# A butterfly FFN behind a gated scan on one core: the down side's high product as whole 128x512 products, its result regrouped by 32 on-chip copies, and one token load issued later

## The chip, the cores and the metric

One Trainium2 chip, one of its cores. The metric is the device time of one execution of the program in microseconds (us), lower is better. The profiled execution gives a time of its own, and a span from its first to its last instruction; all positions in time below count from the start of that span.

## The reference, cut to what matters

```python
# x, ctx: (32, 512, 512) f32; hidden width 2048, 11 butterfly stages
x = x + layernorm(x) * scan(ctx * ctx)            # r = 0.9 * r + kv, along the sequence
h = layernorm(x) @ W_exp + b_exp                  # 512 -> 2048
h = butterfly(h, up_weights)                      # 11 stages of 2x2 blocks, strides 1 .. 1024
h = gelu(h + up_bias)
h = butterfly(h, down_weights)                    # 11 stages
x = x + (h @ W_con + b_con) + down_bias           # 2048 -> 512
```

A butterfly over 2048 features is a low part (7 stages with strides under 128: 16 blocks of 128x128, one a block of features) times a high part (4 stages with strides 128 to 1024, which mix the 16 blocks). Neither depends on the tokens, so the program multiplies both into the weights once, at its start, and then runs all tokens through two dense products.

## The kernel before

**The fold.** The first 140 us make the two dense weight matrices. For the down side the source is `W_con`, loaded into the tile `wcon` as 16 slices `r` of 128 rows (row `(k, e)` of slice r is the feature of block k with rank r and place e within it). Three kinds of fold step work on it, each on TensorE (PE) into one of four PSUM banks in turn, and each followed by an eviction on ScalarE (ACT), line 995:

- `high_dn` r = 0..15 (line 1818): four products with 128x128 output each, of slice r of `wcon` with the high matrix `HX[:, 1, r]`. The result comes out transposed, and the eviction scatters it into the tile `Z`.
- `back` k = 0..15 (line 1824): four 128x128 transposes each that turn block k of `Z` back, evicted into `wcon[:, k]` (two of them on VectorE, DVE, line 1345).
- `low_dn` i = 0..15 (line 1803): one 128x512 product of block `W2_ORDER[i]` of `wcon` with the low matrix `LX[:, 1]`. ACT (line 992) and DVE (line 1341) split the result in two parts, which SyncE (SP) stores to DRAM (line 634) as the tensor `w2_split`.

Between them stand small steps: `tokens` 0..7 (line 1822, transposes of the normalised first tokens, evicted into `raw`), `bias_low` (line 1792), `turn_low` (line 1820, evicted into `LX`). A fold step may begin when the step four before it has been evicted, since it takes its bank.

**The splits of the up side.** `weights_hi(0)` and `weights_hi(1)` on ACT (line 1022) and `weights_lo` on DVE (line 1350) split the first two pairs of up-side weights; SP stores them in three groups each (`store_w1`, line 623). ACT waits for the stores of groups 0 and 1 of the first before it evicts `tokens` 0 (their staging tile lies over `raw`).

**The tokens.** `tokens_hi(0, m)` on ACT (line 1040) and `tokens_lo(0, m)` on DVE (line 1445) split the tokens of product m of 7 into the tile `xop`; `token_sum` (DVE, line 1462) makes the sums for four of them. The tile `xop` lies over the region of `Z`: slot 4 and up of it are used early.

**The steady state.** 32 units of 1024 tokens, each of 8 pairs p; a pair is 7 products m of 6 matmuls (line 1916, a Strassen-like scheme) with down products between (lines 1937, 1950), in an order written out by hand. In unit 0 the products of pair 0 are woven with the last `low_dn` steps, and pairs 2 to 7 take their up weights from "late" loads (lines 655, 656), which are split on ACT and GpSimd (POOL) and stored for the later units. SP issues nearly all transfers, in program order: a wait in it holds all that stands behind. In pair 1 of unit 0 it loads the token rows of unit 1 into `x` (`load_x`, two halves of 1 MB, four transfers each).

Of the kernel before, what the change touches and what calls it, by code (L numbers as in the profile page):

```python
# [24 lines left out]
def xattn_ffn_program(nc, x_in, ctx_in, w_exp, b_exp, up_w, up_bias, down_w, w_con, b_con, down_bias, out):  # L25
# [6 lines left out]
    P = 128  # L32
# [4 lines left out]
    LOW = 7  # L37
# [19 lines left out]
    XORDER = (0, 1, 3, 2, 5, 4, 6)  # L57

# [6 lines left out]
    W2_ORDER = (2, 3, 4, 5, 6, 7, 12, 13, 8, 1, 9, 0, 14, 10, 11, 15)  # L65
    W2_USE = [(i, 0) for i in range(14)] + [(3, 1), (14, 0)]
# [16 lines left out]
    with es:  # L83
# [122 lines left out]

        low_loaded = [sem("low_up_loaded"), sem("low_dn_loaded")]
# [118 lines left out]
        FOLD += [("high_dn", r, "act") for r in range(4)]  # L326
        FOLD += [("bias_low", 0, "act")]
        FOLD += [("high_dn", r, "act") for r in range(4, 8)]
        FOLD += [("bias_turn", 0, "act")]
        FOLD += [("high_dn", r, "act") for r in range(8, R - 3)]  # L330
        FOLD += [("tokens", i, "act") for i in range(2)]
        FOLD += [("high_dn", r, "act") for r in range(R - 3, R)]
        FOLD += [("tokens", i, "act") for i in range(2, J)]
        FOLD += [("turn_low", q, "act") for q in range(KH // 4)]
        FOLD += [("back", k, "act") for k in range(10)]
        FOLD += [("tokens", i, "act") for i in range(J, J + 2)]
        FOLD += [("back", k, "dve" if k in (11, 13) else "act") for k in range(10, KH)]
        FOLD += [("tokens", i, "dve") for i in range(J + 2, 2 * J)]


        FOLD += [("low_dn", k, "dve") for k in range(KH)]
# [78 lines left out]
        Zd = Z[:, :, :].rearrange("p a b -> p (a b)").rearrange("p (c h) -> p c h", c=KD)  # L420

        def kept(kind, i, bank):
# [13 lines left out]
            if kind == "turn_high":  # L436
                return HX[:, 1, 4 * i:4 * i + 4, :].rearrange("p a b -> p (a b)"), whole
# [6 lines left out]
            if kind == "tokens":  # L444
                return raw[:, i // J, :, :].rearrange("p c (g j i) -> p c g j i", g=G, j=J)[:, :, :, i % J, :],\
                    whole.rearrange("p (c g i) -> p c g i", c=KD, g=G)
            assert kind == "back"
            return wcon[:, i, :], whole
# [121 lines left out]
        def _(sp):  # L570
# [48 lines left out]
            def store_w1(n):  # L619
                p = W1_ORDER[n]  # L620
                for g, (m0, m1) in enumerate(GROUPS):
# [19 lines left out]
            store_w1(0)  # L641
# [44 lines left out]
            def load_x(u, par):  # L686
                wait(sp, out_stored, (u - 1) * (2 * G * NX))
                for h in range(2):
                    load_tokens(xs[par], h, x_rows, u * 2 + h, x_loaded[h])

            def body(u, par, first, last):
# [4 lines left out]
                for p in range(NP):  # L696
# [3 lines left out]
                    for m in range(NM):  # L700
# [29 lines left out]
                        if go and p == 1 and m == 5:  # L730
# [3 lines left out]
                            load_x(u + 1, 1 - par)  # L734
# [245 lines left out]
        def _(act):  # L980
# [43 lines left out]
            def tokens_hi(u, m, first):  # L1024
                if not first:
                    act.wait_ge(m_done, u * PER + (m + 1 - NM))
                if m in (0, 1):
                    if first:
                        act.wait_ge(fold_made, fold_at("back", KH - 1) + 1)
# [10 lines left out]
                act.activation(xop[:, XPOS[m], 0, :, :], x_source(m), ACT.Copy).then_inc(xhi_ready, 1)  # L1040
# [48 lines left out]
            fold_step("high_dn", 3)  # L1089
            fold_step("bias_low", 0)  # L1090
            for r in range(4, 8):
                fold_step("high_dn", r)
            fold_step("bias_turn", 0)
            for r in range(8, 12):
                fold_step("high_dn", r)
            fold_step("high_dn", 12)
            for group in range(2):
                act.wait_ge(w1_stored[0][group], NX)
            for i in range(2):
                fold_step("tokens", i)  # L1100
            for r in range(13, R):
                fold_step("high_dn", r)
            for i in range(2, J):
                fold_step("tokens", i)
            for q in range(KH // 4):
                fold_step("turn_low", q)
            for k in range(4):
                fold_step("back", k)
            for k in range(4, 10):
                fold_step("back", k)  # L1110
            for i in range(J, J + 2):
                fold_step("tokens", i)
            for k in (10, 12, 14, 15):
                fold_step("back", k)
            tokens_hi(0, 0, True)
            tokens_hi(0, 1, True)
            for k in range(4):
# [123 lines left out]
        def _(dve):  # L1241
# [73 lines left out]
            def top_products(dn):  # L1315
                dve.wait_ge(path_product, spreads(dn, LOWS - 1))
                for c, bank in enumerate(TOP_PLACE[dn]):
# [3 lines left out]
                    if dn:  # L1321
                        last = nc.vector.tensor_tensor(
                            out=whole.rearrange("p o (r a e) -> p o a e r", r=R, a=2),
                            in0=paths.rearrange("p (o e r) -> p o e r", o=KH // 4, r=R).unsqueeze(2)
                            .to_broadcast([P, KH // 4, 2, E // 2, R]),
                            in1=coef.rearrange("p o a (e r) -> p o a e r", r=R), op=ALU.mult)
                    else:
                        last = path_stage(nc.vector, flat(whole), paths, coef, LOW - 1)
# [114 lines left out]
            def tokens_lo(u, m):  # L1443
                dve.wait_ge(xhi_ready, u * NM + (XPOS[m] + 1))
                nc.vector.tensor_tensor(out=xop[:, XPOS[m], 1, :, :], in0=x_source(m),  # L1445
# [601 lines left out]
```

## Time and profile before

| | |
|---|---|
| time before, median of 3 runs | 2752.51 us (2751.94 to 2758.26) |
| the profiled execution: its time / its span | 2752.11 us / 2750.4 us |
| PE busy (matmul) | 2728.7 us, 99% of the span |
| DVE, ACT, POOL busy | 2119.6, 1132.2, 427.1 us |
| granted TensorE clock, mean | 0.996 of full |
| DMA | 535.76 MB, 195 GB/s over the span |

A share of busy time is an average over stages. The fold (up to 142 us) has other limits than the rest, and it is the part that the change touches, so it is read by itself: by stretches, and by the order of the instructions on each engine.

### The profile page before, as it was taken

The numbers are of one execution on the slowest core, as the hardware profiler recorded it, in microseconds if no ns is written. First come the engines' busy times: TensorE is split into PE (matmuls) and PEld (weight loads), VectorE is DVE, ScalarE is ACT, GpSimd is POOL, SyncE is SP. The second block draws the span as 40 slices with busy tenths as digits, with TensorE's granted clock in tenths as the row PEclk, the third lists the DMA queues.
The fourth block names the chain that finished last, engine by engine and source line by source line (L and its number), as shares of the span: only waits on it lengthen the run. The fifth ranks groups of instructions, "written<-read, shape, count | busy, mean of one in ns | idle before, by whom it ended". The sixth has DMA issues, their size and how long they took to land.

```text
span 2750.4 us, 35138 instructions
## 1 busy us (share of the span) xinstructions
PE 2728.7 (99%) x12168; PEld 2251.9 (82%) x12168; DVE 2119.6 (77%) x3544; ACT 1132.2 (41%) x1731; POOL 427.1 (16%) x608
## 2 busy tenths in 40 slices
PE   8999999999999999999999999999999999999998
PEld 6788888888888888888888888888888888888887
DVE  8888887877878777787877788787787877778533
ACT  5754434344343433434343343434334343343432
POOL 5356010110101011020111101011010101102000
PEclk8999999999999999999999999999999999999999
DMA  9675956657585675857657585675758567585543
GB/s 274 244 235 171 281 165 198 200 170 224 155 231 177 181 220 161 241 153 216 194 168 222 152 249 165 194 202 171 223 156 235 172 189 213 161 242 153 187 146 100
DMA packets 288373, 535.76 MB, mean 195 GB/s; under 512 B 36854, under 2 KB 98454, under 8 KB 271046
## 3 DMA queue, kind: packets, MB, share of 16 engines
q1 hardware_dynamic: 281808, 531.05, 64.1%
q10 hardware_dynamic: 5414, 1.25, 0.3%
q8 instruction: 99, 1.62, 0.2%
q0 software_dynamic: 976, 1.22, 0.2%
q14 instruction: 76, 0.62, 0.1%
HBM read 437.96 MB, written 63.96 MB: 182 GB/s over the span
## 4 chain that ended last, share of the span: by engine, by line
PE 98%; DVE 1%; ACT 0%; issue 0%; DMA 0%; POOL 0%; DVEq 0%
PE ps L1916 44%; PE ps L1937 25%; PE ps L1950 25%; PE ps L1814 1%; PE ps L1710 1%; PE ps L1782 0%; PE ps L1818 0%; PE ps L1812 0%; PE ps L1824 0%; DMA wexp<-in_L_ffn_W_exp_dram 0%; PE ps L2022 0%; PE ps L1803 0%; DVE raw L1462 0%; DVE xop L1445 0%; PE ps L1729 0%
## 5 line engine op out<-in xcount | busy, mean ns | idle before, releaser
L1916 PE MATMUL ps<-xop,w1r 128*128 128x512 f32 x5376 | 1366.1, 389 | 2.4 <-DVE xop L1445 2.4
L1916 PEld LDWEIGHTS ps<-xop,w1r 128*128 128x128 f32 x5376 | 1009.0, 188 | 215.2 <-DVE xop L1445 3.4
L1937 PE MATMUL ps<-w2r,ghi 128*128 128x512 f32 x2048 | 630.5, 389 | 0.0
L1950 PE MATMUL ps<-w2r,ghi 128*128 128x512 f32 x2032 | 625.7, 389 | 1.1 <-DVE x L1544 1.1
L1127 ACT ACTIVATE st<-ps 128x512 f32<-128x512 f32 x384 | 229.6, 598 | 820.0 <-PE ps L1916 819.9
L1544 DVE TENSOR_TENSOR x<-ps,x 128x512 f32<-128x512 f32 x508 | 348.4, 686 | 275.1 <-PE ps L1950 272.7
L1937 PEld LDWEIGHTS ps<-w2r,ghi 128*128 128x128 f32 x2048 | 384.4, 188 | 79.9 <-DVE w2x L1341 0.2
L1950 PEld LDWEIGHTS ps<-w2r,ghi 128*128 128x128 f32 x2032 | 381.3, 188 | 81.0 <-DVE x L1544 2.0
L1562 DVE TENSOR_TENSOR g<-ps,st 128x512 f32<-128x512 f32 x384 | 262.5, 684 | 211.7 <-PE ps L1916 211.7
L1131 ACT ACTIVATE g<-g,gelu_bias 128x512 f32<-128x512 f32 x384 | 275.5, 717 | 353.0 <-DVE g L1562 352.9
L1567 DVE TENSOR_TENSOR glo<-g,ghi 128x512 fp32r<-128x512 f32 x510 | 350.9, 708 | 72.8 <-ACT ghi L1145 72.8
L1937 PE MATMUL ps<-w2r,glo 128*128 128x512 f32 x1024 | 398.3, 389 | 0.0
L1950 PE MATMUL ps<-w2r,glo 128*128 128x512 f32 x1016 | 395.2, 389 | 0.0
L1145 ACT ACTIVATE ghi<-g 128x512 fp32r<-128x512 f32 x512 | 309.8, 629 | 12.2
L1138 ACT ACTIVATE g<-ps,gelu_bias 128x512 f32<-128x512 f32 x128 | 88.2, 689 | 349.0 <-PE ps L1916 349.0
L1937 PEld LDWEIGHTS ps<-w2r,glo 128*128 128x128 f32 x1024 | 192.3, 188 | 39.8
L1950 PEld LDWEIGHTS ps<-w2r,glo 128*128 128x128 f32 x1016 | 190.8, 188 | 39.5
L836 POOL TENSOR_TENSOR x<-x,bias_row 128x512 f32<-128x512 f32 x128 | 170.0, 1332 | 244.2 <-DVE kvT L1434 218.8
L819 POOL TENSOR_TENSOR ve<-mv,eps 128x4 f32<-128x4 f32 x32 | 12.2, 382 | 1197.2 <-DVE mv L1385 1197.2
L1371 DVE TENSOR_TENSOR_SCAN kvT<-decay,kvT 128x512 f32<-128x512 f32 x128 | 159.1, 1243 | 4.4
L1445 DVE TENSOR_TENSOR xop<-raw,xop 128x1024 fp32r<-128x1024 f32 x112 | 136.6, 1232 | 0.7 <-ACT xop L1040 0.7
L827 POOL TENSOR_TENSOR ve<-mv,eps 128x1 f32<-128x1 f32 x128 | 28.2, 220 | 597.8 <-DVE mv L1413 597.8
(182 smaller groups left out, 1700.0 us busy)
## 6 DMA issues: line engine op xcount, KB each, us to landing
w1r<-w_products SPq DMA_DIRECT2D x847, 256.0 KB, 3.3
w2r<-w_split SPq DMA_DIRECT2D x126, 1024.0 KB, 5.0
x<-in_x_dram SPq DMA_DIRECT2D x128, 256.0 KB, 7.0
raw<-kv SPq DMA_DIRECT2D x480, 64.0 KB, 2.1
out_dram<-x SPq DMA_DIRECT2D x120, 256.0 KB, 4.1
kv<-in_ctx_dram SPq DMA_DIRECT2D x64, 256.0 KB, 7.4
raw<-in_ctx_dram SPq DMA_DIRECT2D x64, 256.0 KB, 5.0
w_products<-w1r SPq DMA_DIRECT2D x43, 256.0 KB, 6.9
```

Of the source, the lines that this page charges most:

```text
L836: nc.gpsimd.tensor_tensor(out=x[:, J * h + j, :], in0=x[:, J * h + j, :], in1=bias_row[:, :], op=ALU.add).then_inc(bias_added, 1)
L1127: act.activation(st[:, i, :], bank[:, :], ACT.Copy).then_inc(copied, 1)
L1131: act.activation(g32[:, q, :], g32[:, q, :], ACT.Gelu, bias=gelu_bias[:, k:k + 1])\
L1145: act.activation(ghi[:, p % 2, q, :], g32[:, q, :], ACT.Copy).then_inc(ghi_ready, 1)
L1371: nc.vector.tensor_tensor_scan(out=flat, data0=decay[:, :], data1=flat, initial=0.0, op0=ALU.mult, op1=ALU.add).then_inc(scanned, 1)
L1445: nc.vector.tensor_tensor(out=xop[:, XPOS[m], 1, :, :], in0=x_source(m), in1=xop[:, XPOS[m], 0, :, :].bitcast(f32), op=ALU.subtract).then_ ...
L1544: nc.vector.tensor_tensor(out=x[:, J + j, :], in0=ps_yb[:, :], in1=x[:, J + j, :], op=ALU.add)\
L1562: nc.vector.tensor_tensor(out=by_chunk(g32[:, q, :]), in0=by_token(bank[:, :]), in1=by_token(st[:, i, :]), op=ALU.add).then_inc(h_ready, 1)
L1567: nc.vector.tensor_tensor(out=glo[:, p % 2, q, :], in0=g32[:, q, :], in1=ghi[:, p % 2, q, :].bitcast(f32), op=ALU.subtract).then_inc(glo_r ...
L1916: last = nc.tensor.matmul(bank[:, :], w1r[:, slot, w, c * P:(c + 1) * P], xop[:, XPOS[m], v, c, :], start=(opens and i == 0), stop=(i == l ...
L1937: last = nc.tensor.matmul(ps_ya[j][:, :], g[:, p % 2, q, j * P:(j + 1) * P], w2r[:, p % 2, kk, w, :], start=(p == 0 and kk == 0 and i == 0 ...
L1950: last = nc.tensor.matmul(ps_yb[:, :], g[:, p % 2, q, j * P:(j + 1) * P], w2r[:, p % 2, kk, w, :], start=(kk == 0 and i == 0), stop=(kk == ...
```

## The change

The four 128x128 products of a `high_dn` step become one 128x512 product with the operands the other way round, so its result is not transposed any more, and is evicted as it is into `Z[:, r]`. The 16 `back` steps with their evictions are gone. What `back` did to the places of the rows is done by DMA: for each r one copy takes 64 partitions of `Z[:, r]` (half the blocks; 2 KB of each partition, 128 KB in all) to 8 partitions r, r+16, ... of `wcon`, 8 blocks of 2 KB each. There are 32 such copies on SP's queue: 16 for blocks 0 to 7 (after `high_dn` 7 has read its slice and step r has been evicted), and 16 for blocks 8 to 15 (after `high_dn` 15). `low_dn` 0 waits for the first 16, `low_dn` 6 for the other 16. The stores of the first pair's up weights are taken apart: group 1 after nine copies, group 2 after all 32.

`tokens` 0..7 are all evicted by ACT now; `bias_low` and `bias_turn` come after all `high_dn`; the first three `tokens_hi` come earlier on ACT. The slots of `xop` are dealt out anew (`XSLOT`), and the slots over `Z` wait for its copies.

Apart from that, the second half of `load_x` in unit 0 is issued at m = 3 of pair 2 instead of at m = 5 of pair 1, so behind the stores and loads of late weights that stand between.

```diff
     XORDER = (0, 1, 3, 2, 5, 4, 6)
+    XSLOT = (5, 6, 1, 0, 3, 2, 4)
...
+    LOW_BLOCKS_FIRST = 6
...
             if kind == "high_dn":
-                return Zd[:, :, :].rearrange("p c (k r e) -> p c k r e", k=KH, r=R)[:, :, :, i, :],\
-                    whole.rearrange("p (c k e) -> p c k e", c=KD, e=E)
+                return Z[:, i, :], whole
...
+            def move_dn(blocks, r, moved):
+                wait_kept(sp, "high_dn", r)
+                sp.dma_start(wcon[r:P:R, blocks, :], Z[blocks.start * E:blocks.stop * E, r, :]).then_inc(moved, NX)
...
-            store_w1(0)
+            store_w1(0, range(1))
+            sp.wait_ge(fold_made, fold_at("high_dn", R // 2 - 1) + 1)
+            for r in range(R):
+                move_dn(slice(0, KH // 2), r, dn_low_moved)
+                if r == R // 2:
+                    store_w1(0, range(1, 2))
+            sp.wait_ge(fold_made, fold_at("high_dn", R - 1) + 1)
+            for r in range(R):
+                move_dn(slice(KH // 2, KH), r, dn_top_moved[r // 4])
+            store_w1(0, range(2, NG))
...
-                            load_x(u + 1, 1 - par)
+                            load_x(u + 1, 1 - par, range(1) if first else range(2))
+                        if first and p == 2 and m == 3:
+                            load_x(u + 1, 1 - par, range(1, 2))
...
+                if first and XSLOT[m] < R // 4:
+                    act.wait_ge(dn_low_moved, R * NX)
+                    act.wait_ge(dn_top_moved[XSLOT[m]], 4 * NX)
+                if first and m == 6:
+                    act.wait_ge(w1_stored[0][2], NX)
...
                 if kind == "low_dn":
                     k = W2_ORDER[i]
-                    wait_kept(pe, "back", k)
+                    if i == 0:
+                        pe.wait_ge(dn_low_moved, R * NX)
+                    if i == LOW_BLOCKS_FIRST:
+                        for moved in dn_top_moved:
+                            pe.wait_ge(moved, 4 * NX)
...
+                if kind == "high_dn":
+                    nc.tensor.matmul(bank[:, :], HX[:, 1, i, :], wcon[:, i, :], start=True, stop=True).then_inc(fold_made, 1)
+                    return
...
                 if first:
-                    for k in range(4):
+                    for k in range(2, 4):
                         fold_step("low_dn", k)
                     product(u, 0, 0, first)
-                    for k in range(4, 6):
-                        fold_step("low_dn", k)
                     product(u, 0, 1, first)
-                    for k in range(6, 8):
+                    for k in range(4, 8):
                         fold_step("low_dn", k)
                     product(u, 0, 2, first)
```

On PE, from the `high_dn` steps to the first `low_dn`, the order before (`HX,wcon` are `high_dn`, `ident,Z` are `back`, `wcon,LX` are `low_dn`, `ident,kv` are `tokens`, `ident,LX` are `turn_low`, `LX,scr` is `bias_low`):

```order
L1818 MATMUL ps<-HX,wcon 128x128 x16
L1792 MATMUL ps<-LX,scr 16x128 x16
L1818 MATMUL ps<-HX,wcon 128x128 x16
L1798 MATMUL ps<-ident,scr 128x16
L1818 MATMUL ps<-HX,wcon 128x128 x20
L1822 MATMUL ps<-ident,kv 128x128 x8
L1818 MATMUL ps<-HX,wcon 128x128 x12
L1822 MATMUL ps<-ident,kv 128x128 x8
L1820 MATMUL ps<-ident,LX 128x128 x16
L1824 MATMUL ps<-ident,Z 128x128 x40
L1822 MATMUL ps<-ident,kv 128x128 x8
L1824 MATMUL ps<-ident,Z 128x128 x24
```

The same place of the changed program (`wcon,HX` are `high_dn`):

```order
L1800 MATMUL ps<-wcon,HX 128x512 x16
L1816 MATMUL ps<-ident,kv 128x128 x16
L1781 MATMUL ps<-LX,scr 16x128 x16
L1814 MATMUL ps<-ident,LX 128x128 x16
L1787 MATMUL ps<-ident,scr 128x16
L1796 MATMUL ps<-wcon,LX 128x512 x2
L1816 MATMUL ps<-ident,kv 128x128 x16
L1796 MATMUL ps<-wcon,LX 128x512 x2
L1899 MATMUL ps<-xop,w1r 128x512 x12
L1796 MATMUL ps<-wcon,LX 128x512 x4
L1899 MATMUL ps<-xop,w1r 128x512 x6
```

The 64 transposes of `back` are gone, all `high_dn` stand in one run, and the last four `tokens` have moved behind the first two `low_dn`. After the third product the order is as before.

On SP, from the store of the folded up weights to the first store of `w_split`, before:

```order
L639 DMA w_folded<-W1f 128x3072 x2
L623 DMA w_products<-w_first 128x2x512
L623 DMA w_products<-w_first 128x512
L623 DMA w_products<-xop 128x4x512
L609 DMA w1r<-w_products 128x512
L623 DMA w_products<-w1r 128x2x512
L623 DMA w_products<-w1r 128x512
L623 DMA w_products<-w1r 128x4x512
L634 DMA w_split<-w2s 128x2x512
```

and in the changed program:

```order
L636 DMA w_folded<-W1f 128x3072 x2
L620 DMA w_products<-w_first 128x2x512
L613 DMA wcon<-Z 8x8x512 x9
L620 DMA w_products<-w_first 128x512
L613 DMA wcon<-Z 8x8x512 x23
L620 DMA w_products<-xop 128x4x512
L601 DMA w1r<-w_products 128x512
L620 DMA w_products<-w1r 128x2x512
L620 DMA w_products<-w1r 128x512
L620 DMA w_products<-w1r 128x4x512
L631 DMA w_split<-w2s 128x2x512
```

The 32 copies stand between the stores, and every later transfer of the fold is queued behind them.

## Rows read from the trace of the kernel before

**Rows 1.** The page: span, busy time of each engine.

```profile
span 2750.4 us, 35138 instructions
PE 2728.7 (99%) x12168; PEld 2251.9 (82%) x12168; DVE 2119.6 (77%) x3544; ACT 1132.2 (41%) x1731; POOL 427.1 (16%) x608
```

**Rows 2.** Stretches of the start: busy time by engine, granted clock, DMA share, GB/s.

```profile
core 0: us, PE busy (x) PEld busy (x) DVE busy (x) ACT busy (x) POOL busy (x), PEclk, DMA share, GB/s
79.00:101.00 22.00, 21.37 (x187) 20.41 (x187) 21.25 (x36) 17.06 (x34) 11.14 (x13) 1.00 0.82 314
101.00:112.00 11.00, 11.00 (x92) 9.71 (x91) 5.55 (x12) 10.74 (x22) 6.45 (x28) 1.00 0.01 1
112.00:142.00 30.00, 26.73 (x85) 15.12 (x84) 27.18 (x34) 21.41 (x36) 6.34 (x4) 1.00 0.79 266
```

**Rows 3.** PE from 79 to 142 by line: count | busy us, mean ns | idle.

```profile
L1803 PE MATMUL ps<-wcon,LX 128*128 128x512 f32 x32 | 15.3, 602 | 0.8 <-DVE w2s L1341 0.6
L1818 PE MATMUL ps<-HX,wcon 128*128 128x128 f32 x128 | 15.2, 277 | 0.2 <-ACT HX L995 0.2
...
L1824 PE MATMUL ps<-ident,Z 128*128 128x128 f32 x64 | 7.8, 281 | 0.0
L1822 PE MATMUL ps<-ident,kv 128*128 128x128 f32 x32 | 4.3, 276 | 0.0
L1792 PE MATMUL ps<-LX,scr 128*16 128x128 f32 x32 | 3.7, 273 | 0.4 <-ACT Z L995 0.4
```

**Rows 4.** PE in order of time: start, us, line, count [idle before it].

```profile
79.30 3.81 PE L1818 MATMUL ps<-HX,wcon 128*128 128x128 f32 x32 [0.22 <-ACT HX L995]
...
96.48 2.84 PE L1818 MATMUL ps<-HX,wcon 128*128 128x128 f32 x24
...
111.12 3.60 PE L1803 MATMUL ps<-wcon,LX 128*128 128x512 f32 x8
...
119.70 1.12 PE L1803 MATMUL ps<-wcon,LX 128*128 128x512 f32 x2
...
127.46 3.59 PE L1803 MATMUL ps<-wcon,LX 128*128 128x512 f32 x8
130.89 0.29 PE L1983 MATMUL ps<-scr 128*128 128x16 f32 x2
...
139.64 1.61 PE L1916 MATMUL ps<-xop,w1r 128*128 128x512 f32 x6
...
211.16 0.73 PE L1950 MATMUL ps<-w2r,ghi 128*128 128x512 f32 x2 [0.46 <-DVE x L1544]
```

**Rows 5.** ACT in order of time, two evictions of high_dn steps.

```profile
82.88 1.55 ACT L995 ACTIVATE Z<-ps 128x512 f32<-128x512 f32 x3
...
87.03 0.58 ACT L995 ACTIVATE Z<-ps 128x512 f32<-128x512 f32 x1
```

**Rows 6.** DVE in order of time: first token_sum; statistics of the second half.

```profile
114.36 1.22 DVE L1462 TENSOR_TENSOR raw<-raw 128x1024 f32<-128x1024 f32 x1
...
215.72 2.46 DVE L1392 BATCH_NORM_STATS2 st<-x 128x6 f32<-128x512 f32 x4
```

**Rows 7.** DMA rates of three stretches, columns as in rows 2.

```profile
82.00:84.00 2.00, 1.59 (x15) 1.35 (x15) 1.93 (x3) 2.00 (x4) 1.92 (x2) 1.00 1.05 442
...
157.00:166.00 9.00, 9.00 (x41) 7.44 (x41) 8.79 (x15) 5.78 (x9) 2.58 (x3) 1.00 1.07 246
...
262.00:272.00 10.00, 10.00 (x45) 8.29 (x45) 5.96 (x7) 5.40 (x11) 8.68 (x7) 1.00 0.43 110
```

**Rows 8.** SP's queue: start, us spent issuing, transfer, count.

```profile
261.86 10.69 SPq L566 DMA_DIRECT2D raw<-kv  x16
```

**Rows 9.** DMA issues: KB each, median us from issue to landing.

```profile
raw<-kv SPq DMA_DIRECT2D x480, 64.0 KB, 2.1
```

**Rows 10.** Two stretches early in the start-up, columns as in rows 2.

```profile
12.00:14.00 2.00, 0.29 (x3) 0.05 (x1) 2.00 (x3) 2.00 (x5) 2.00 (x2) 1.00 1.11 289
...
17.00:24.00 7.00, 7.00 (x24) 5.38 (x23) 6.38 (x11) 4.43 (x6) 7.00 (x17) 0.53 1.10 223
```

More of the change, by code:

```diff
@@ L205, in xattn_ffn_program @@
         ps_f = ps[5:8]
+        dn_low_moved = sem("dn_low_moved")
+        dn_top_moved = [sem(f"dn_top_moved{q}") for q in range(R // 4)]
         low_loaded = [sem("low_up_loaded"), sem("low_dn_loaded")]
@@ L325, in xattn_ffn_program @@
         FOLD += [("turn_high", q, "act") for q in range(R // 4)]
-        FOLD += [("high_dn", r, "act") for r in range(4)]
+        FOLD += [("high_dn", r, "act") for r in range(R)]
+        FOLD += [("tokens", i, "act") for i in range(J)]
         FOLD += [("bias_low", 0, "act")]
-        FOLD += [("high_dn", r, "act") for r in range(4, 8)]
+        FOLD += [("turn_low", q, "act") for q in range(KH // 4)]
         FOLD += [("bias_turn", 0, "act")]
[L330 to L341, printed above, removed]
+        FOLD += [("low_dn", k, "dve") for k in range(2)]
+        FOLD += [("tokens", i, "act") for i in range(J, 2 * J)]
+        FOLD += [("low_dn", k, "dve") for k in range(2, KH)]
         kept_count, kept_so_far = [], {"act": 0, "dve": 0}
@@ L418, in w1_columns @@
             return w[:, :, :, r * E:(r + 1) * E].rearrange("p k c e -> p c k e")
-        Zd = Z[:, :, :].rearrange("p a b -> p (a b)").rearrange("p (c h) -> p c h", c=KD)
         def kept(kind, i, bank):
@@ L443, in kept @@
                     whole.rearrange("p (a e r) -> p a r e", a=4, e=E)
[L444 to L448, printed above, removed]
+            assert kind == "tokens"
+            return raw[:, i // J, :, :].rearrange("p c (g j i) -> p c g j i", g=G, j=J)[:, :, :, i % J, :],\
+                whole.rearrange("p (c g i) -> p c g i", c=KD, g=G)
         def w2_slot(i):
@@ L1320, in top_products @@
                     coef = spread_view(ps[bank][:, :], 0, LOW - 1, KH // 4)
[L1321 to L1328, printed above, removed]
+                    last = path_stage(nc.vector, flat(whole), paths, coef, LOW - 1)
                 last.then_inc(low_matrix_ready, 1)
@@ L1507, in _ @@
                 normalise(0, 1, xs[0], j)
-            for k in (11, 13):
-                fold_step("back", k)
-            for i in range(J + 2, 2 * J):
-                fold_step("tokens", i)
             tokens_lo(0, 0)
             tokens_lo(0, 1)
-            token_sum(0, 0, first=True)
             for k in range(2):
                 fold_step("low_dn", k)
+            token_sum(0, 0, first=True)
             token_sum(0, 1)
@@ L1877, in _ @@
                 fold_step("turn_low", q)
-            wait_kept(pe, "high_dn", R - 2)
-            wait_kept(pe, "high_dn", R - 1)
-            for k in range(KH):
-                if k == 10:
-                    for i in range(J, J + 2):
-                        fold_step("tokens", i)
-                fold_step("back", k)
-            for i in range(J + 2, 2 * J):
+            fold_step("bias_turn", 0)
+            wait_kept(pe, "turn_low", KH // 4 - 1)
+            for k in range(2):
+                fold_step("low_dn", k)
+            for i in range(J, 2 * J):
                 fold_step("tokens", i)
-            wait_kept(pe, "turn_low", KH // 4 - 1)
             def product(u, p, m, first):
```

67 lines of the change are left out of this document (23 added, 44 removed).

## The prediction

> **What bounds the kernel now.** I read the page first, then the stretches of the start, then each engine there in order of time. PE is busy for 99% of the span [rows 1], so the steady state gives and takes nothing: whatever this change does happens in the start-up, where the fold runs. By stretches [rows 2], PE works 21.4 of 22 us from 79 to 101 and all of 101 to 112, so PE itself is the limit there; from 112 to 142 it works 26.7 of 30, with DVE at 27.2 of 30, so there DVE sets the pace. The DMA engines are idle from 101 to 112 (share 0.01) and loaded on both sides of it (0.82 and 0.79). The marks on PE to hold a new schedule against are [rows 4]: first `high_dn` at 79.30, last one done at 96.48 + 2.84 = 99.3, `low_dn` 0 at 111.12, `low_dn` 6 at 119.70, first product of pair 1 at 139.64. The change of the last mark is the change of the kernel's time, unless something behind it stalls.
>
> **What PE loses and gains.** By the groups of lines [rows 3], the 64 transposes of `back` cost 7.8 us and go. The 64 small `high_dn` products cost 15.2 us. Sixteen 128x512 products replace them; four `low_dn` products of that shape take 130.89 - 127.46 = 3.43 us [rows 4], 0.857 us each, so 13.7 us. The ceiling of the gain is 7.8 + 1.5 = 9.3 us.
>
> The steps are now packed tighter than their evictions come. Step 4 needs the bank of step 0, whose eviction begins at 82.88 behind `weights_hi(0)` and ends near 83.4 [rows 5], while PE would be ready at 79.30 + 3.43 = 82.7: a wait of 0.7 us. Step 7 needs the eviction of step 3, which stands behind `weights_hi(1)` and ends at 87.03 + 0.58 = 87.6 [rows 5]; PE is ready at 83.4 + 2.6 = 86.0: 1.6 us. Then nine steps at 0.857: the last `high_dn` ends at 95.3, 4.0 us earlier than before. With durations from [rows 3], four `tokens` (half of 4.3 us for eight, less where they are pipelined, 1.8) end at 97.1, `bias_low` (3.7) at 100.8, `turn_low` (some 1.9) at 102.7; its last eviction on ACT stands behind a `tokens_hi` and ends near 104.3. So without any wait for copies `low_dn` 0 starts at 104.3, 6.8 us early. Then come two `low_dn` (1.7) and the last four `tokens` (1.8) with their evictions; the first `token_sum` on DVE can start near 108.8, where it starts at 114.36 now [rows 6]. From there DVE has the same list as before, and it is the limit, so 5.5 us is what arrives at pair 1.
>
> **The copies.** There are 32, of 128 KB each, on SP's queue, 4.2 MB in all. The first can be issued once step 7 is made, at 87.6 + 0.9 = 88.5. A copy of this kernel from SBUF to SBUF (`raw<-kv`, 64 KB, 32 partitions to 32) lands 2.1 us after its issue [rows 9]; its transfer is 0.27 us of that (below), so 1.8 us is fixed. On SP one such issue costs 10.69 / 16 = 0.67 us [rows 8]; 32 take 21 us, to about 110.
>
> How long the transfer of one copy takes is shown by no row, and the whole case hangs on it. The nearest rows [rows 7]: transfers over 128 partitions move 442 GB/s at a DMA share of 1.05; loads of token rows into 32 partitions at a time, among others, move 246 GB/s at a share of 1.07; the `raw<-kv` copies move 110 GB/s at a share of 0.43, so 10 x 0.43 / 16 = 0.27 us of all engines for 64 KB. At 442 GB/s a copy takes 0.30 us, the lower bound. Like `raw<-kv` it takes 0.54 us. The rows also say that at a full share the rate halves nearly (442 to 246) when a transfer writes 32 partitions in place of 128. A copy here writes 8. If the rate halves once more (123 to 110 GB/s) a copy takes 1.06 to 1.2 us; if it falls in proportion to the partitions (62 GB/s) 2.1 us, the upper bound. The form of the access (8 target partitions, in steps of 16) is further from `raw<-kv` than that is from a full tile, so I take a further halving, at its slow end, 1.2 us.
>
> The Trainium skill, page "SBUF — State Buffer", section "Door 1: The DMA port swizzle", says that SBUF is reached through 16 ports, chosen by bits 2 to 4 and 6 of the partition number, each about 27 GB/s. By it the targets r, r+16, ... of one copy reach four ports, some 109 GB/s, 1.2 us a copy; the row of `raw<-kv` would have 0.54 us and the kernel 5.5 us faster, the page has it slower. The loads into 32 partitions in the trace agree with it (8 ports), and no row here shows four. The page "DMA: Bandwidth & Descriptors", section "Why a DMA increments its semaphore by 16 and not by 1", adds that a transfer is split over as many engines as divide its outermost sizes, here 8; that alone would make 0.6 us.
>
> **Who waits for them.** At 1.2 us a copy, with the 256 KB store of group 1 between them (0.65 us at 400 GB/s):
> - Group 1 lands at 88.5 + 1.8 + 9 x 1.2 + 0.65 = 101.8. ACT waits for it ahead of the eviction of `tokens` 0, and PE's `bias_low` for that bank: `bias_low` from 102.3 to 106.0, `turn_low` evicted at 109.5.
> - The low 16 land at 88.5 + 1.8 + 19.2 + 0.65 = 110.2: `low_dn` 0 starts there, 0.9 us earlier than before.
> - The top 16 land at 110.2 + 19.2 = 129.4. `low_dn` 6 waits for all of them; PE reaches it at about 120 and stands for 9 us, and behind it stand products 2 to 6 and all other `low_dn`, while DVE runs out of work.
> - From `low_dn` 6 to pair 1 the order is unchanged and takes 139.64 - 119.70 = 19.9 us now, 0.6 of it a wait that falls away [rows 4]: 19.3. Pair 1 starts at 129.4 + 19.3 = 148.7, 9.1 us later than now.
>
> Each 0.1 us on a copy moves this by 3.2 us. The two chains (copies; PE and DVE) meet at 0.9 us a copy for no change, and below 0.72 the 5.5 us are kept whole.
>
> Two smaller terms. The group 2 store, the stores of the second pair's weights and 16 stores of `w_split` (8.4 MB) start after the copies, at 129 and not at 116, with pair 1 only 9 us later; the loads of late weights behind them lose some 4 us of their lead. And PE stands still for 9 us: in the start-up PE was busy for 0.3 us of 12 to 14, and over 17 to 24 the granted clock was 0.53 [rows 10], so mostly the lower of its two levels (1.2 of 2.4 GHz); the same over a few us of this dense stretch costs 1 to 3 us. I add 2 us for both (0 to 5).
>
> **The second edit.** Four 256 KB transfers move from behind the first half in pair 1 to behind the late loads of pair 2. With pair 1 at 148.7 and a pair of 20 us (three and a half of them from 139.64 to 211.16 [rows 4]) they are issued near 177. DVE reads this half at 215.72 [rows 6], 39 us after that, so it costs nothing; if that cover were gone it would cost the 4.3 us that 1 MB takes at 246 GB/s [rows 7]. It frees the queue for the split weights and late weights of pairs 2 and 3, which is worth something only if PE waits for them; the one PE wait in that part is 0.46 us, for DVE [rows 4]. I take 0.
>
> **Sum**, against the profiled execution (2752.11 us, span 2750.4 [rows 1], 1.7 us outside it): 2752.1 + 9.1 + 2 = 2763.2. The median of the runs is 2752.51, so I say 2763. About 0.3% (8.3 us, so 2760.8 and 2744.3) is what a measurement here tells from no change.
>
> **Rivals.**
> - *The copies are quick enough* (up to 0.72 us, like `raw<-kv`, or only half the engines' rate). For it: that row is the one on-chip copy in the trace; against it: eight target partitions. Then `low_dn` 0 is at 104.3, `low_dn` 6 near 114.5 with the top copies landed at 88.5 + 1.8 + 32 x 0.67 + 0.65 = 112.4, and the time 2752.1 - 5.5 = 2746.6. Decides below 0.9 us a copy. Chance 0.34.
> - *In between* (0.8 to 1.0 us): 2749 to 2756. Chance 0.12.
> - *The backlog decides*: as forecast, but the queue behind the copies starves pairs 1 and 2 (split and late weights land late), or a copy takes 1.4 us and more. For it: the DMA engines have a share of 1.07 from 157 to 166 already [rows 7]. Then 8 us and more on top: 2771 and up. Chance 0.10.
> - *The forecast*: copies of 1.06 to 1.28 us, small terms 0 to 5: 2757 to 2769. Chance 0.44.
>
> **The numbers.** The forecast's own range lies above 2760.8 for about six sevenths: slower 0.38 + 0.10 = 0.48. Faster by over 8.3 us needs nearly the whole ceiling of 9.3 us and no new wait: 0.04. The rest, 0.48, is within. To hold eight in ten the range goes from the quick case (2745) to the foot of the backlog case (2771).
>
> **What would show it.** The 16 `high_dn` products end near 95.3 in any case, with two waits of 0.7 and 1.6 us for ACT among them. SP issues the copies from 88.5 at 0.6 to 0.7 us. In the stretch 92 to 108 the DMA rate is 100 to 125 GB/s if I am right, over 180 if the quick case holds. `low_dn` 0 starts near 110 (or 104), and PE's longest wait of the start is at `low_dn` 6, some 9 us (or none). Pair 1 starts at 148.7 to 151 (or near 134). I am wrong if copies overlap where I have them share a limit, or if the stores between them were the real wait.

## The result, and the profile of the changed kernel

The changed kernel takes 2763.69 us (median of 5 runs, 2762.59 to 2765.66); the kernel before, on the same chip, 2751.94 us (5 runs, 2751.2 to 2758.26). The ratio is 1.0039, with a 95% interval of 1.0025 to 1.0054: 11.8 us slower, where 2763 was forecast. The profiled execution has a span of 2762.0 us.

TensorE in order of time, the changed kernel (start, us, line, count, idle before it in brackets; line 1800 is `high_dn`, 1816 `tokens`, 1781 `bias_low`, 1796 `low_dn`, 1899 the products of the tokens; each `low_dn` step leaves two records, so x4 is two steps):

```profile
78.16 3.67 PE L1800 MATMUL ps<-wcon,HX 128*128 128x512 f32 x8 [0.22 <-ACT HX L1003]
82.71 2.81 PE L1800 MATMUL ps<-wcon,HX 128*128 128x512 f32 x6 [0.87 <-ACT Z L1003]
87.06 7.96 PE L1800 MATMUL ps<-wcon,HX 128*128 128x512 f32 x18 [1.54 <-ACT Z L1003]
94.86 1.91 PE L1816 MATMUL ps<-ident,kv 128*128 128x128 f32 x16
102.95 5.82 PE L1781 MATMUL ps<-LX,scr 128*16 128x128 f32 x32 [6.18 <-ACT raw L1003]
...
111.99 1.98 PE L1796 MATMUL ps<-wcon,LX 128*128 128x512 f32 x4 [1.16 <-ACT scr L1003]
...
128.94 3.75 PE L1796 MATMUL ps<-wcon,LX 128*128 128x512 f32 x4 [6.70 <-DMA wcon<-Z]
133.87 2.93 PE L1899 MATMUL ps<-xop,w1r 128*128 128x512 f32 x6 [1.18 <-DVE xop L1438]
...
137.52 2.24 PE L1899 MATMUL ps<-xop,w1r 128*128 128x512 f32 x6
...
144.59 1.66 PE L1899 MATMUL ps<-xop,w1r 128*128 128x512 f32 x6 [1.27 <-DVE xop L1438]
...
151.79 1.63 PE L1899 MATMUL ps<-xop,w1r 128*128 128x512 f32 x6
```

The last row is the first product of pair 1. It stood at 139.64 [rows 4]; it is 12.15 us later, and the whole kernel 11.8 us: in this kernel all of the loss arises in the start, none of it behind. The row of 128.94 is `low_dn` 6, which stands 6.70 us for the copies. And the engine is slow behind it: two `low_dn` steps (four records) take 3.75 us there, and 1.98 at 111.99.

The rows alone could mislead on the other large wait, 6.18 us ahead of `bias_low`. The row of ACT that it waits for, and SP's queue over the same time:

```profile
102.30 2.06 ACT L1003 ACTIVATE raw<-ps 128x512 f32<-128x512 f32 x4 [6.64 <-DMA w_products<-w_first]
```

```profile
88.19 5.89 SPq L613 DMA_DIRECT2D wcon<-Z  x9
94.12 0.56 SPq L620 DMA_DIRECT2D w_products<-w_first  x1
94.74 18.23 SPq L613 DMA_DIRECT2D wcon<-Z  x23
113.02 0.83 SPq L620 DMA_DIRECT2D w_products<-xop  x1
```

The store of group 1 is issued at 94.12, but ACT, which waits for it, starts only at 102.30: nine copies are ahead of it. Experiment 9 shows that this wait costs nothing.

By stretches (columns as in [rows 2]), the changed kernel:

```profile
79.00:101.00 22.00, 15.36 (x47) 7.15 (x45) 21.01 (x37) 13.22 (x24) 11.59 (x14) 0.99 0.63 206
...
96.00:100.00 4.00, 0.77 (x8) 0.53 (x5) 3.82 (x8) 0.00 (x0) 3.08 (x4) 1.00 0.53 105
104.00:108.00 4.00, 4.00 (x23) 2.93 (x22) 1.22 (x1) 1.42 (x2) 0.00 (x0) 0.58 0.53 116
108.00:112.00 4.00, 2.84 (x26) 2.32 (x23) 1.23 (x1) 3.19 (x7) 0.00 (x0) 1.00 0.53 121
124.00:128.00 4.00, 0.00 (x0) 0.00 (x0) 0.00 (x0) 0.00 (x0) 0.00 (x0) 0.56 0.87 265
128.00:132.00 4.00, 3.06 (x4) 1.17 (x4) 0.00 (x0) 0.98 (x2) 0.00 (x0) 0.50 0.97 375
132.00:136.00 4.00, 2.82 (x6) 1.75 (x6) 3.41 (x4) 1.54 (x3) 0.00 (x0) 0.50 1.05 371
136.00:142.00 6.00, 6.00 (x16) 3.35 (x16) 3.45 (x6) 3.38 (x5) 0.00 (x0) 0.82 0.98 365
142.00:160.00 18.00, 16.71 (x65) 11.58 (x64) 14.20 (x20) 13.46 (x22) 6.35 (x4) 1.00 1.02 320
```

The copies move 105 to 121 GB/s at a DMA share of 0.53. 131,072 bytes at these rates are 1.25 to 1.08 us a copy; by the landing, (128.94 - 88.19 - 1.8 - 0.65) / 32 = 1.20 us. The share says that the 16 engines as a whole are half free in the stretches from 96 to 112, in which the copies run nearly alone. It doesn't say so any more while TensorE waits at `low_dn` 6 (0.87 from 124 to 128, at 265 GB/s): by then the stores and loads behind the copies are moving as well. After TensorE's wait the granted clock is 0.50, the lower level (1.2 GHz), until about 138.

### The profile page after: what moved, and what is told of

Same layout as the page of the kernel before. It is cut to its first block, busy times and chain, and to the rows that moved or that the text cites. A ratio compares the mean times of both kernels' runs of the same rounds, so it can differ in the third digit from the quotient of the medians.

```text
span 2762.0 us, 34825 instructions
## 1 busy us (share of the span) xinstructions
PE 2726.1 (99%) x12008; PEld 2238.6 (81%) x12008; DVE 2115.7 (77%) x3540; ACT 1126.5 (41%) x1719; POOL 431.7 (16%) x608
## 3 DMA queue, kind: packets, MB, share of 16 engines
q10 hardware_dynamic: 5414, 1.25, 0.3%
## 4 chain that ended last, share of the span: by engine, by line
PE 97%; DMA 1%; ACT 0%; DVE 0%; POOL 0%; issue 0%; SPq 0%; ACTq 0%; DVEq 0%
PE ps L1899 44%; PE ps L1920 25%; PE ps L1933 25%; DMA wcon<-Z 1%; PE ps L1699 1%; PE ps L1810 1%; PE ps L1771 0%; DMA w_products<-w_first 0%; PE ps L1808 0%; PE ps L1796 0%; PE ps L1800 0%; PE ps L1781 0%; PE ps L2003 0%; DMA wexp<-in_L_ffn_W_exp_dram 0%; PE ps L1718 0%
## 5 line engine op out<-in xcount | busy, mean ns | idle before, releaser
L827 POOL TENSOR_TENSOR ve<-mv,eps 128x4 f32<-128x4 f32 x32 | 11.8, 369 | 1198.0 <-DVE mv L1378 1198.0
```

## The experiments

The theory: a copy takes 1.2 us because its 8 target partitions, in steps of 16, are written at some 110 GB/s; the landing of the last 16 holds `low_dn` 6, and from there to pair 1 the order takes its 19.9 us and some for the clock. Its rivals: the wait for the store of group 1 is the loss; the copies share a limit that has nothing to do with the targets (8 engines, SP's issues); the queue behind them is what costs. Ratios are to the kernel before on the same chip.

**1 and 2: each edit alone.** The second edit alone is the kernel before with

```diff
-                            load_x(u + 1, 1 - par)
+                            load_x(u + 1, 1 - par, range(1) if first else range(2))
+                        if first and p == 2 and m == 3:
+                            load_x(u + 1, 1 - par, range(1, 2))
```

> The kernel before with the second edit alone: the second half of unit 1's token rows is issued at m = 3 of pair 2 behind the late weights. My account: no effect, within 1 us of the kernel before (2752), pair 1 starts at 139 to 140 as before, and no new wait of PE. Rival (the second edit carries part of the 12 us, because the load then collides with the loads of late weights): 2754 to 2764 and new PE waits between 142 and 230.

2751.86 us, ratio 0.9995 (0.9986 to 1.0004): nothing. The copies alone are the changed kernel with these lines turned back.

> The changed kernel without the second edit: only the fold is changed. My account: all of the loss is in the fold, so the time is that of the changed kernel, 2762 to 2765, with PE's wait of 6 to 7 us for the top copies. Rival (the second edit is needed to keep the token rows from the late weights once the queue is 13 us behind): over 2766, with PE waits in pairs 1 to 3. Other rival (the second edit costs): below 2760.

2769.8 us (2765.53 to 2771.07), ratio 1.0059 (1.0046 to 1.0073). Pair 1 starts where it does with both edits (151.22), so the other 5.7 us (17.4 against 11.8 over before) are lost behind it. The profile of the copies alone is of an execution of 2765.53 us, the quickest of the five, and shows only a part of that: TensorE is busy for 18.35 of 20 us from 180 to 200, in pair 2 (all 20 in the changed kernel), and ahead of that stands ACT's wait for the late weights that are queued behind the two megabytes of token rows:

```profile
188.87 0.73 ACT L1154 ACTIVATE w1r<-late_top 128x256 fp32r<-128x256 f32 x2 [6.69 <-DMA late_low<-w_folded]
```

So the second edit is worth nothing by itself and 5.7 us in this kernel.

**3: half the bytes.** Each copy moves the first 1 KB of each row and not the 2 KB, so half of the down side's weights is not regrouped (its product is not the reference's); the count of copies stays.

```diff
-                sp.dma_start(wcon[r:P:R, blocks, :], Z[blocks.start * E:blocks.stop * E, r, :]).then_inc(moved, NX)
+                sp.dma_start(wcon[r:P:R, blocks, 0:D // 2], Z[blocks.start * E:blocks.stop * E, r, 0:D // 2]).then_inc(moved, NX)
```

> The changed kernel with the 32 copies moving only the first 1 KB of each 2 KB row (half of what low_dn then reads is left as loaded from W_con). Same count of copies, same issue time on SP, same waits. If the transfer time of the copies is what holds PE (1.16 us a copy), it falls to about 0.6 us, no wait for the top copies is left, and the time is 2745 to 2750. If SP's issuing (0.6 us each) or a fixed cost of each copy is what counts, the copies end no more than a few us earlier and the time stays at 2758 or above.

2749.98 us, ratio 0.9988 (0.9979 to 0.9997). No wait for copies is left, and pair 1 starts at 136.42, 3.2 us earlier than before. The bytes are the cost, not the number of issues. And the best that the idea has to give, with half of its transfers for nothing, is 2.4 us.

**4 and 5: other target partitions.** In steps of 4, with the columns of the low matrix in the matching order, so that the result is the same product:

```diff
-                sp.dma_start(wcon[r:P:R, blocks, :], Z[blocks.start * E:blocks.stop * E, r, :]).then_inc(moved, NX)
+                at = Q * (r % 4) + r // 4
+                sp.dma_start(wcon[at:at + Q - 3:4, blocks, :], Z[blocks.start * E:blocks.stop * E, r, :]).then_inc(moved, NX)
```

> The changed kernel with each copy's eight target partitions in steps of 4 and not of 16 (rows of each block stored in another order, and the low matrix written in the same order by the DVE operation that makes it): same bytes, same count of copies, of rows and of target partitions. If the targets share ports by pairs (four ports for steps of 16, eight for steps of 4), a copy takes about 0.6 us, DMA rate 200 to 220 GB/s in the stretch of the copies, low_dn 0 starts near 104, no long wait for the top copies, and the time is 2745 to 2749, faster than both kernels. If the limit is the number of target partitions or the source side (64 partitions), nothing changes: 105 to 120 GB/s and 2762 to 2765.

2753.31 us, ratio 1.0002 (0.9993 to 1.0011). The stretches of this kernel:

```profile
104.00:108.00 4.00, 3.17 (x26) 2.52 (x24) 1.75 (x2) 2.85 (x6) 0.00 (x0) 0.96 0.51 180
108.00:112.00 4.00, 3.58 (x19) 2.33 (x20) 1.38 (x2) 2.59 (x7) 3.13 (x18) 1.00 0.51 182
...
142.00:160.00 18.00, 16.15 (x71) 12.76 (x70) 11.99 (x19) 9.16 (x15) 6.77 (x8) 1.00 1.04 322
```

180 GB/s in place of 116 to 121, at the same share: as much of the DMA engines is held, for a shorter time (0.73 us a copy). The wait at `low_dn` 6 is gone and pair 1 starts at 138.25. TensorE then loses 1.85 us in 142 to 160 that the kernel before doesn't lose.

Side by side, with the regrouped product in the wrong order:

```diff
-                sp.dma_start(wcon[r:P:R, blocks, :], Z[blocks.start * E:blocks.stop * E, r, :]).then_inc(moved, NX)
+                sp.dma_start(wcon[E * r:E * (r + 1), blocks, :], Z[blocks.start * E:blocks.stop * E, r, :]).then_inc(moved, NX)
```

> The changed kernel with each copy written to 8 partitions side by side (8r to 8r+7) in place of 8 in steps of 16; the same bytes, source, count of copies, and queue. The regrouped product is then in the wrong order, so the output is not the reference's; the work on every engine is the same. Theory 1, the place of the targets sets the rate of a copy: side by side they reach fewer ports than in steps of 16 (by the Trainium skill, page "SBUF - State Buffer", section "Door 1: The DMA port swizzle", two, 54 GB/s), so a rate of 50 to 60 GB/s in the stretch 96 to 112 at the same share of 0.53, some 2.3 us a copy, the top copies landed near 88.5 + 1.8 + 32 x 2.3 + 0.65 = 165 and pair 1 at 165 + 20 to 23 = 185 to 188, the kernel some 35 us slower than the changed one (2795 to 2802). Theory 2, the number of target partitions (8) sets it, or that 8 of the 16 engines do the work: 105 to 121 GB/s as in the changed kernel, and 2763 to 2765.

2776.93 us in its one run. The stretches of this kernel:

```profile
104.00:108.00 4.00, 0.00 (x0) 0.00 (x0) 0.07 (x1) 0.00 (x0) 0.00 (x0) 0.50 0.54 68
...
112.00:116.00 4.00, 4.00 (x20) 2.87 (x19) 1.23 (x1) 1.65 (x3) 0.00 (x0) 0.50 0.54 93
```

`low_dn` 6 starts at 142.87, (142.87 - 89.13 - 1.8 - 0.65) / 32 = 1.60 us a copy; 62 to 68 GB/s in the stretches from 92 to 108 that hold no store, 93 to 94 from 112 to 124. The place of the targets does set the rate, in the direction expected, but 2.3 us was too much, and why the rate rises from 68 to 93 on the way was not found. One reading is that neighbouring copies overlap where their targets differ enough. That became the tenth experiment.

**6: TensorE kept busy.** Eight products more, thrown away, ahead of the wait at `low_dn` 6:

```diff
+                        for _ in range(8):
+                            nc.tensor.matmul(ps_yb[:, :], LX[:, 1, k, :], wcon[:, W2_ORDER[0], :], start=True, stop=True)
```

> The changed kernel with 8 products of 128x512 (results thrown away) on TensorE between low_dn 5 and the wait of low_dn 6. Theory 1, of the 22.9 us from low_dn 6 to pair 1 (19.3 at the pace of before) some 3 us are the granted clock of 0.50 after the wait: busy for 6.9 of the 6.7 us of the wait, the engine keeps a clock near 1, low_dn 6 starts no later (129 to 130), pair 1 at 148.5 to 149.5 in place of 151.8, and the kernel 2760 to 2762. Theory 2, the 3 us come from something else (ACT or DVE behind late stores): the clock after low_dn 6 is higher, but pair 1 stays at 151 to 152 and the time at 2763 to 2764. If the products run at the lower clock themselves they take up to 14 us and low_dn 6 starts up to 7 us later: then the time is over 2765 and the run tells nothing on the clock.

2763.94 us, ratio 1.0043 (1.0029 to 1.0056): no difference from the changed kernel that can be told. In its profile the clock is 1.00 when `low_dn` 6 starts, at 131.29 (the whole start stands later, first `high_dn` at 79.94), and pair 1 follows 21.55 us later, not 22.85. So 1.3 of the 3 us over 19.9 go with the clock of the first steps. The clock falls again, to 0.50 from 136 to 138, after TensorE has waited 2.03 us for DVE:

```profile
131.29 1.96 PE L1798 MATMUL ps<-wcon,LX 128*128 128x512 f32 x4 [0.45 <-DMA wcon<-Z]
135.28 2.53 PE L1901 MATMUL ps<-xop,w1r 128*128 128x512 f32 x6 [2.03 <-DVE xop L1438]
...
138.53 2.29 PE L1901 MATMUL ps<-xop,w1r 128*128 128x512 f32 x6
```

The same two products in the kernel before:

```profile
123.72 1.67 PE L1916 MATMUL ps<-xop,w1r 128*128 128x512 f32 x6 [1.16 <-DVE xop L1445]
...
125.68 1.94 PE L1916 MATMUL ps<-xop,w1r 128*128 128x512 f32 x6
```

From the start of the one to the start of the other it is 1.96 us before, 3.25 us here and 3.65 in the changed kernel, with no wait between in any of them. So most of the rest is the lower clock too.

**7 and 8: what remains with quick copies.** With steps of 4, the store of group 1 ahead of all copies:

```diff
-            store_w1(0, range(1))
+            store_w1(0, range(2))
...
-                if r == R // 2:
-                    store_w1(0, range(1, 2))
```

> The kernel with target partitions in steps of 4 (2753.3), and the store of group 1 issued ahead of the copies, no longer between them. Theory 1, that store's place costs ACT its 2.7 us wait ahead of bias_low: the wait is gone, low_dn 0 starts at 105 to 106 in place of 108.3, and if nothing else holds, pair 1 at 135.5 in place of 138.25 and the kernel 2750 to 2751. Theory 2, the DMA queue behind the copies is the limit by then (a share of 1.04 from 116 to 160): low_dn 0 is early all the same, but the 2.7 us are given back at ACT's wait for the context rows and DVE's behind it (142 to 165), and the kernel stays at 2752.5 to 2754.

2753.24 us, ratio 1.0004 (0.9995 to 1.0013). And on top of it, the loads of unit 1's context rows ahead of the first five stores of `w_split`; its old place in pair 0 is empty:

```diff
             store_w1(1)
+            sp.wait_ge(fold_made, fold_at("tokens", 2 * J - 1) + 1)
+            load_tokens(kv, 0, ctx_rows, 2, ctx_loaded[0])
             for i in range(5):
                 store_w2(i)
```

> As the kernel with steps of 4 and the store first, and the four loads of unit 1's context rows issued ahead of the first five stores of w_split, not behind ten of them. Theory 1, what is left of the loss is that ACT waits 3.7 us for these rows at 144.8: the wait falls below 1 us, PE's waits at 153 and 160 (1.8 us) shrink, and the kernel is 1 to 3 us faster than the one with the store first (2748 to 2751). Theory 2, the queue as a whole is late, so that whichever transfer stands last is waited for: then the first five w_split stores land 4 us later, DVE and ACT wait for their buffers from 120 to 140, and the time is the same or up to 3 us worse.

2752.85 us, ratio 1.0003 (0.9994 to 1.0012). ACT in the kernel with the store first, and then in the one with the context rows earlier too:

```profile
145.28 1.92 ACT L1006 ACTIVATE kv<-kv 128x2048 f32<-128x2048 f32 x1 [4.51 <-DMA kv<-in_ctx_dram]
...
151.45 0.72 ACT L1130 ACTIVATE g<-g,gelu_bias 128x512 f32<-128x512 f32 x1 [3.77 <-DMA w_split<-w2s]
```

```profile
135.10 0.18 ACT L1190 ACTIVATE gelu_bias<-ps 128x16 f32<-128x16 f32 x1 [3.49 <-DMA w_split<-w2s]
```

The wait of 4.51 us for the context rows is gone in the second, and the wait for `w_split` stands at 135 and not at 151; TensorE, which started pair 1 at 137.87 in the first, starts it at 141.93 here. The time is the same. That is how a full queue looks (DMA share 0.97 to 1.05 from 116 to 160 in both): putting one transfer ahead makes another the late one.

**9: the store of group 1 first, slow copies.** The two edits of the diff of the seventh, in the changed kernel:

> The changed kernel with the store of group 1 issued ahead of the copies, targets in steps of 16 as in the change. Theory 1, only the landing of the top copies decides: the wait ahead of bias_low (6.2 us) is gone, low_dn 0 waits for the low copies instead, until about 109, the wait at low_dn 6 stays near 6.7 us or grows, and the top copies land at the same place (128 to 129, 0.65 us earlier at most): the time stays at 2762.5 to 2764. Theory 2, the 6.2 us wait of ACT and TensorE ahead of bias_low is part of the loss: pair 1 starts up to 6 us earlier (146 to 148) and the time is 2757 to 2759.

2764.22 us, ratio 1.0043 (1.0029 to 1.0056), as the changed kernel. TensorE:

```profile
97.53 3.67 PE L1779 MATMUL ps<-LX,scr 128*16 128x128 f32 x32
...
110.86 3.75 PE L1794 MATMUL ps<-wcon,LX 128*128 128x512 f32 x4 [7.61 <-DMA wcon<-Z]
...
129.17 3.75 PE L1794 MATMUL ps<-wcon,LX 128*128 128x512 f32 x4 [5.97 <-DMA wcon<-Z]
```

The 6.18 us ahead of `bias_low` are gone, and 7.61 us at `low_dn` 0 have taken their place; `low_dn` 6 starts at 129.17 as at 128.94. Of two waits in a row, the one that ends last counts. Pair 1 is at 150.05 in this profile, 20.88 us behind `low_dn` 6 and not 22.85: the granted clock was back at 1.00 by 134 to 136 here, where it was 0.50 until 138 in the changed kernel.

**10: the same copies in another order.** The changed kernel with

```diff
-            for r in range(R):
+            turns = [8 * a + b + c for a in range(2) for b in range(4) for c in (0, 4)]
+            for n, r in enumerate(turns):
                 move_dn(slice(0, KH // 2), r, dn_low_moved)
-                if r == R // 2:
+                if n == R // 2:
...
-            for r in range(R):
+            for r in turns:
                 move_dn(slice(KH // 2, KH), r, dn_top_moved[r // 4])
```

> The changed kernel with the copies issued in the order r = 0, 4, 1, 5, 2, 6, 3, 7, 8, 12, 9, 13, 10, 14, 11, 15 in both halves and nothing else: each copy has the same bytes, shape and targets as before. By the port rule of the Trainium skill (page "SBUF - State Buffer", section "Door 1: The DMA port swizzle") copies r and r + 4 write to different ports, copies r and r + 1 (r in the same four) to the same ones. Theory 1, what sets the rate is which ports are written at one time, and neighbouring copies overlap: 150 to 180 GB/s in the stretch 96 to 112, some 0.75 us a copy, no wait at low_dn 6, pair 1 near 138 to 140 and the kernel at 2752 to 2755. Theory 2, each copy by itself is held to the rate of its own four ports, or to something in its shape that the order doesn't change: 105 to 121 GB/s, a wait of 6 to 7 us at low_dn 6, 2763 to 2764.

2754.42 us, ratio 1.0007 (0.9998 to 1.0016): some 10 us of the 11.8 are back, and nothing but the order of 32 issues has changed. Stretches and the place of `low_dn` 6 and pair 1 in this kernel:

```profile
92.00:96.00 4.00, 4.00 (x11) 1.67 (x10) 3.82 (x8) 2.88 (x5) 1.44 (x2) 1.00 0.55 125
96.00:100.00 4.00, 1.90 (x17) 1.66 (x15) 3.81 (x10) 0.60 (x1) 2.60 (x5) 1.00 0.61 157
...
104.00:108.00 4.00, 4.00 (x27) 2.94 (x25) 1.22 (x1) 1.15 (x2) 0.00 (x0) 0.69 0.52 176
108.00:112.00 4.00, 2.85 (x20) 2.29 (x20) 1.23 (x1) 3.19 (x7) 0.63 (x4) 1.00 0.53 202
```

```profile
119.60 3.75 PE L1797 MATMUL ps<-wcon,LX 128*128 128x512 f32 x8
...
141.16 1.63 PE L1900 MATMUL ps<-xop,w1r 128*128 128x512 f32 x6
```

No wait is left at `low_dn` 6. A copy in steps of 16 is not held to 105 to 121 GB/s by itself; a row of them to neighbouring partitions is. The 4.77 us wait ahead of `bias_low` is still there; the eleventh experiment asks whether it counts now.

**11 and 12: two variations of the tenth.** With the store of group 1 first (the edit of the seventh):

> The changed kernel with the copies in turns (r, r + 4) and the store of group 1 ahead of them. Theory 1, with quick copies the 4.8 us wait ahead of bias_low is on the path as far as PE and DVE are, until the queue behind the copies decides: low_dn 0 at 106 to 107 in place of 111.2, pair 1 at 138 to 139 in place of 141.2, but ACT then waits longer for the context rows and w_split (4 us and more, in place of 1.7 and 2.7), and the time is 2752.5 to 2754 (as with steps of 4 and the store first, 2753.2). Theory 2, the queue is not the limit: the 3 us arrive whole and the time is 2751 to 2752.

2752.68 us, ratio 1.0002 (0.9993 to 1.0010). The time is the one expected, the way to it is not: `low_dn` 0 is at 108.33, held 3.90 us by the copies, and pair 1 at 140.48. The 4.77 us at `bias_low` were worth some 1 us: this kernel is 0.9 us over the kernel before, the tenth 1.8, which the intervals don't tell apart. It is level with the kernel before; no version here that does the whole work beats it.

With no store between the copies this kernel shows their rate cleanly:

```profile
96.00:100.00 4.00, 4.00 (x31) 3.16 (x30) 3.81 (x10) 3.50 (x7) 2.75 (x3) 1.00 0.53 125
100.00:104.00 4.00, 4.00 (x38) 3.56 (x36) 3.86 (x10) 2.33 (x4) 2.58 (x4) 1.00 0.53 130
104.00:108.00 4.00, 0.43 (x4) 0.17 (x2) 2.60 (x3) 1.59 (x5) 2.11 (x8) 0.84 0.53 168
108.00:112.00 4.00, 3.67 (x5) 1.53 (x6) 0.69 (x1) 0.60 (x1) 3.06 (x18) 0.50 0.53 203
```

The ninth kernel, with the same place of the store and the copies in order, has 101, 109, 113 and 115 GB/s in these stretches. So turns help the first copies by only a fifth and nearly double the rate of the last ones; why it takes so long to rise was not found. That is why `low_dn` 0 still waits here: (108.33 - 90.19 - 1.8) / 16 = 1.02 us for each of the first 16 copies.

The other is the tenth with the second edit turned back:

> The changed kernel with the copies in turns and without the second edit (both halves of unit 1's token rows in pair 1, as before the change). Theory 1, the second edit is worth something because the queue behind the copies is full, whatever the copies' own rate: the DMA share is above 1 from 116 to 160 here too, TensorE loses 2 to 4 us in pairs 1 and 2 that it does not lose with the edit, and the kernel is at 2757 to 2760. Theory 2, it is worth 6 us only where the copies are slow and everything stands 12 us later: with quick copies the time stays within 1 us of the kernel with both edits (2753.5 to 2755.5), as the edit alone did nothing (2751.9).

2757.19 us, ratio 1.0021 (1.0012 to 1.0030). Against the kernel before on the same chip it is 5.4 us slower, the tenth 1.8: the second edit is worth 3.5 us with quick copies as well. ACT in this kernel, at the place of the wait in the second experiment (the tenth kernel has no such wait there; TensorE is busy for 18.92 of 20 us from 180 to 200 here and for all 20 in the tenth):

```profile
178.84 0.72 ACT L1155 ACTIVATE w1r<-late_top 128x256 fp32r<-128x256 f32 x2 [6.12 <-DMA late_low<-w_folded]
```

## Why the prediction was right, by its steps

**What TensorE loses and gains: right.** From the first `high_dn` to the end of the last the changed kernel takes 95.02 - 78.16 = 16.9 us (16.0 forecast), with waits of 0.87 and 1.54 us for ACT (0.7 and 1.6). The start as a whole stood 1.1 us earlier in this execution than in the one of before; the other kernels here have the first `high_dn` at 78.4 to 80.2, so that is scatter.

**A copy takes 1.2 us: right in size, and that it holds `low_dn` 6 is shown; the reason was wrong.** Half the bytes, other targets and another order each take the wait at `low_dn` 6 away. The step was "is further from `raw<-kv` than that is from a full tile, so I take a further halving, at its slow end". The size held (1.20 us) with a share of luck: eight target partitions, the reason given, are the same in the fourth and fifth experiments, which took 0.73 and 1.60 us a copy. The rate depends on which partitions are written, by one copy and over a run of neighbouring copies (101 to 121 GB/s in order; in turns 125 at first and 203 at the end, with the same eight targets a copy). The Trainium skill, page "SBUF — State Buffer", section "Door 1: The DMA port swizzle", gives the ports from bits 2 to 4 and 6 of the partition number: by it the copies r = 0 to 3 write to the same four, r = 4 to 7 to four others. The three patterns come in the order that this gives: side by side 62 to 94 GB/s, steps of 16 105 to 121, steps of 4 about 180. By the same section 8 ports would allow some 218 GB/s, and two some 54 (an estimate from its 27.2 GB/s a port); the measured 180 is under the one and 62 to 94 over the other, and the measurement decides. So it does for the sentence of the prediction by which the loads into 32 partitions agree with 8 ports: the stretch it reads moved 246 GB/s, over the 218, with other transfers among them. That ports are the mechanism is argued from the three patterns and the order; no run here shows a port, and the slow first half of the copies in turns has no explanation by it.

**Who waits: right.** Group 1 landed at 102.3 (101.8 forecast), the top copies at 128.9 (129.4). TensorE reached `low_dn` 6 at 122.2, 2 us later than forecast, so its wait was 6.7 us and not 9; both end with the copies. Why 2 us later: `bias_low` ran for 5.8 us where 3.7 was forecast, at a granted clock of 0.58 after its own wait. `low_dn` 0 waited for ACT's evictions and not for the low copies, at 112.0 and not 110.2. Neither moved the landing of the top copies, as the ninth experiment shows for the wait ahead of them.

**From `low_dn` 6 to pair 1: mis-sized by 0.6.** I took 19.3 us, less a 0.6 us wait that would fall away. With the clock at 1 and quick copies it takes 19.93 us (seventh experiment, 117.94 to 137.87): a longer wait for DVE's `xop` takes its place.

**The small terms, +2: right in sum.** Measured are 22.85 - 19.94 = 2.9 us over the pace of before, and they are the clock, inside the 1 to 3 us that the prediction gave it. From `low_dn` 6 to the next product it is 4.93 us (4.02 before; two `low_dn` steps took 3.75 us here, and 1.98 at 111.99), from there to the product at 137.52 it is 3.65 (1.96 before, no wait in either), and from there to the one at 144.59 it is 7.07 (6.77): 0.9 + 1.7 + 0.3, at a granted clock of 0.50 until 138. Neither TensorE nor ACT nor DVE waits for a transfer between 129 and 151. Pair 1 stood at 151.79, and 148.7 + 2 was forecast.

**The second edit, 0: wrong.** The step "which is worth something only if PE waits for them; the one PE wait in that part is 0.46 us, for DVE" read the trace of before for a queue that the first edit was about to fill. Alone it is worth 0, with slow copies 5.7 us, with quick ones 3.5. The sum came out right because it gave the backlog behind pair 1 next to nothing (2 us with the clock) and the edit against it nothing at all: two errors of one size that cancel, which is luck. The rival "backlog decides" (2771 and up) is what the copies alone nearly give, 2769.8.

## What to carry to other kernels

A transfer's place in the sum needs two numbers, its bytes over the rate for its shape, and which transfers are next to it: here a reordering of 32 issues, with not a byte changed, was worth 10 us. Look at the DMA share over the stretch in which the transfers that are waited for run alone, and not at the wait itself: at 0.53 the shape or order of the transfers was the limit here, and it could be mended. At the wait the share was 0.87 already, filled by what was queued behind. Where it is 1.0 and over with nothing slow in front, the queue was the limit, and moving one transfer ahead only moved the wait. And price two edits of one change together where they share a queue: cover that the trace of before shows may be used up by the other edit.

## What was not expected of the hardware

- Copies from SBUF to 8 partitions hold the DMA engines at a share of 0.48 to 0.55 whatever their rate (62 to 203 GB/s).
- Copies to partitions r and r + 1 (in steps of 16) in a row move 101 to 121 GB/s; the same copies in turns of r and r + 4 move 125 at first and 203 GB/s in the end.
- Waits of 6 to 8 us on TensorE were each followed by a granted clock of 0.50 to 0.58 (`bias_low` took 5.82 us behind its wait, and 3.67 us in the ninth experiment without it).
